# Experts of a mixture layer: 39 tiles of 128 rows in place of 23 tiles of 256

## The reference

```
logits = xf @ Wr.T                       # 2048 tokens, 8 experts
scores, expert = top_k(logits, 2)
weights = softmax(scores)
for e in range(8):
    h = silu(xf @ Win[e].T)              # 256 -> 512
    y += gate[:, e:e+1] * (h @ Wout[e].T)  # 512 -> 256
```

## Time and profile before

| | |
|---|---|
| median of the runs | 1393.06 us |
| span of the profiled execution | 1390.6 us |
| experts: first transpose to last matmul | 1229.8 to 1365.1 us |
| matmuls recorded in all | 8885 |
| granted TensorE clock, mean | 0.969 |

### The profile page before, as it was taken

How to read it: one execution, slowest core, us unless ns; L and a number is a source line. 1 busy time by engine, 2 the same in 40 slices (tenths; PEclk the granted TensorE clock), 3 DMA queues, 4 the chain that set the end, 5 groups by cost and what they waited for, 6 DMA issues and landing times. The chain is left out here.

```text
span 1390.6 us, 30539 instructions
## 1 busy us (share of the span) xinstructions
PE 1286.4 (93%) x8885; PEld 938.2 (67%) x8885; DVE 1054.3 (76%) x2477; ACT 925.3 (67%) x3621; POOL 743.8 (53%) x1099
## 2 busy tenths in 40 slices
PE   3899999999996999999999999999899999669992
PEld 2234444544345888888888888888787878559992
DVE  6456666666676888888888889888788888746664
ACT  1245555454567899899988998899788878323331
POOL 2354646464646556655665566556455788313331
PEclk9799999999998999999999999999999999879996
DMA  5442323233212202202220122112221101522325
GB/s 136 114 76 56 72 55 68 60 59 70 47 51 65 80 2 81 81 13 67 80 80 23 57 80 80 31 48 80 81 81 54 40 32 36 232 88 78 93 82 184
DMA packets 145819, 100.49 MB, mean 72 GB/s; under 512 B 68541, under 2 KB 139198, under 8 KB 145728
## 3 DMA queue, kind: packets, MB, share of 16 engines
q1 hardware_dynamic: 134592, 87.28, 23.5%
q0 software_dynamic: 3744, 8.45, 1.7%
q10 hardware_dynamic: 7392, 3.64, 0.9%
HBM read 58.42 MB, written 42.48 MB: 73 GB/s over the span
## 5 line engine op out<-in xcount | busy, mean ns | idle before, releaser
L1430 POOL TENSOR_TENSOR head_rstd<-head_rstd,minus_half 128x4 f32<-128x4 f32 x192 | 224.8, 1171 | 15.1
L1418 ACT ACTIVATE squares<-ps 128x128 bf16<-128x128 f32 x768 | 201.8, 284 | 46.3 <-PE ps L1381 36.5
L1381 PE MATMUL ps<-w_proj_in,xq 128*128 128x512 f16 (+1 forms) x1024 | 210.1, 328 | 7.0 <-ACT headsT L1454 6.4
L1510 POOL TENSOR_TENSOR prob<-prob,rinv 128x512 f32<-128x512 f32 x128 | 138.4, 1081 | 107.7 <-DVE rinv L1505 107.4
L1497 ACT ACTIVATE prob<-ps,nmax 128x128 f32<-128x128 f32 x512 | 182.2, 390 | 10.3 <-DVE nmax L1488 9.0
L1454 ACT ACTIVATE headsT<-ps,l_hln 128x256 f32<-128x256 f32 (+1 forms) x256 | 167.8, 688 | 31.7 <-PE ps L1445 31.7
L1418 ACT ACTIVATION_READ_ACCUMULATOR squares<-ps 128x1 f32 x768 | 165.2, 216 | 0.0
L1438 DVE TENSOR_TENSOR heads_n<-ps,head_rstd 128x512 f32<-128x512 f32 x192 | 131.3, 684 | 25.0 <-POOL head_rstd L1430 24.8
L728 DVE TENSOR_REDUCE nmax<-ps 128x4 f32<-128x512 f32 x128 | 85.1, 683 | 73.2 <-PE ps L721 73.0
L1481 PE MATMUL ps<-headsT 128*128 128x128 f32 x1024 | 136.5, 276 | 1.0 <-DVE probT L1526 0.4
L1381 PEld LDWEIGHTS ps<-w_proj_in,xq 128*128 (+1 forms) x1024 | 100.5, 98 | 53.9 <-issue 8.2
(11 more groups left out here) (304 smaller groups left out, 2797.3 us busy)
## 6 DMA issues: line engine op xcount, KB each, us to landing
slots<-blank_slot SPq DMA_DIRECT2D x12, 1554.0 KB, 8.8
halves<-half_made SPq DMA_DIRECT2D x32, 256.0 KB, 2.6
w_proj_in<-halves SPq DMA_DIRECT2D x16, 512.0 KB
taken<-slots SPq DMA_DIRECT2D x23, 259.0 KB, 2.8
w_out_raw<-in_wprojT SPq DMA_DIRECT2D x8, 512.0 KB, 3.8
half_raw<-in_winT SPq DMA_DIRECT2D x16, 256.0 KB, 3.0
half_raw<-in_woutT SPq DMA_DIRECT2D x16, 256.0 KB, 3.1
q_stack<-q_parts SPq DMA_DIRECT2D x48, 64.0 KB
```

The source lines that it names most:

```text
L1381: last = e.matmul(out, xq[:, k, which, slot_at], weights(k, hl, c0, n), start=(k == 0 and hl == 0), stop=(k == KD - 1 and hl == 1))
L1418: last = e.activation(squares[:, 4 * n + h, :], A[n][:, h * HD1:(h + 1) * HD1], ACT.Square, scale=HD1**-0.5, accum_out=hss[:, 4 * n + h:4 ...
L1430: e.tensor_tensor(hr[:, four], hr[:, four], t["half"][:, four], ALU.pow).then_inc(g_r[n].sem, 1)
L1510: e.tensor_tensor(prob[:, kind, :, :], prob[:, kind, :, :], spread(rinv[:, kind, :], P), ALU.mult).then_inc(g_p[kind].sem, 1)
```

## The change

`TS` becomes 1, so a tile has 128 rows and there are 2 x 16 + 7 = 39 tiles. A tile's inner layer (4 x 128 columns) now fits one PSUM bank, so four tiles have a bank each, with one activation, one cast and one subtraction of 512 columns a tile. `hidden` runs two tiles ahead of `down` in place of one. `xT`, `h32` and `hh` have four places, the rings of `taken`, `y` and the notes six. The tables of tiles grow from 24 to 40 entries (three words of experts to five), by `TILES`.

```
-TS = 2
+TS = 1
-    RING = 3
+    RING, DEEP = 6, 4
-    xT = sb("slotsT", [P, 2, 2 * KD, TR], F16)
-    h32, hh = sb("h32", [P, 2, KF, TR]), sb("hidden", [P, 2, 2, KF, TR], F16)
+    xT = sb("slotsT", [P, DEEP, 2 * KD, TR], F16)
+    h32, hh = sb("h32", [P, DEEP, KF, TR]), sb("hidden", [P, DEEP, 2, KF, TR], F16)
...
         def hidden(n):
             e.wait_ge(s_xT, n + 1)
+            if n >= len(Hb):
+                e.wait_ge(s_h, n - len(Hb) + 1)
             mine = expert(n)
             for m in range(KF):
-                if n >= 2 and m % 2 == 0:
-                    e.wait_ge(s_h, 2 * (n - 2) + m // 2 + 1)
...
-                        last = e.matmul(Hb[2 * (n % 2) + m // 2][:, m % 2 * TR:(m % 2 + 1) * TR], w,
-                                        xT[:, n % 2, part * KD + k, :],
+                        last = e.matmul(Hb[n % len(Hb)][:, m * TR:(m + 1) * TR], w, xT[:, n % DEEP, part * KD + k, :],
...
-                if m % 2:
-                    last.then_inc(s_H, 1)
+            last.then_inc(s_H, 1)

         def down(n):
             mine = expert(n)
             if n >= 2:
                 e.wait_ge(s_y, n - 1)
-            for h in range(TS):
-                for m in range(KF):
-                    if h == 0 and m % 2 == 0:
-                        e.wait_ge(s_hh, 4 * n + 2 * (m // 2) + 2)
+            e.wait_ge(s_hh, 2 * n + 2)
+            for m in range(KF):
...
-        turn(0)
-        turn(1)
+        for n in range(3):
+            turn(n)
         e.wait_ge(t["weights_in"], 16 * 2 * LOADS)
         hidden(0)
+        hidden(1)
         for n in range(TILES):
-            if n + 1 < TILES:
-                hidden(n + 1)
             if n + 2 < TILES:
-                turn(n + 2)
+                hidden(n + 2)
+            if n + 3 < TILES:
+                turn(n + 3)
             down(n)
...
-        lift(0)
-        lift(1)
+        for n in range(3):
+            lift(n)
         for n in range(TILES):
             parts(n)
             aim(n)
+            if n + 3 < TILES:
+                lift(n + 3)
...
+        silu(0)
+        silu(1)
+        for n in range(TILES):
             if n + 2 < TILES:
+                silu(n + 2)
```

More of the change, by code:

```diff
@@ L2181, in down @@
                 e.wait_ge(s_y, n - 1)
-            for h in range(TS):
-                for m in range(KF):
-                    if h == 0 and m % 2 == 0:
-                        e.wait_ge(s_hh, 4 * n + 2 * (m // 2) + 2)
[L2186 to L2189, removed]
+            e.wait_ge(s_hh, 2 * n + 2)
+            for m in range(KF):
+                for part, hl in ((0, 0), (0, 1), (1, 0)):
+                    w = wout[:, hl, bass.ds(mine, 1), m, :].rearrange("p e n -> p (e n)")
+                    last = e.matmul(Yb[n % 2][:, 0:D], hh[:, n % DEEP, part, m, :], w,
+                                    start=(m == 0 and part == hl == 0), stop=(m == KF - 1 and part == 1))
             last.then_inc(s_Y, 1)
-        turn(0)
-        turn(1)
+        for n in range(3):
+            turn(n)
         e.wait_ge(t["weights_in"], 16 * 2 * LOADS)
         hidden(0)
+        hidden(1)
         for n in range(TILES):
-            if n + 1 < TILES:
-                hidden(n + 1)
             if n + 2 < TILES:
-                turn(n + 2)
+                hidden(n + 2)
+            if n + 3 < TILES:
+                turn(n + 3)
             down(n)
@@ L2206, in lift @@
             e.wait_ge(s_turn, n + 1)
-            if n >= 2:
-                e.wait_ge(s_H, 2 * (n - 1))
-            e.tensor_copy(xT[:, n % 2, :, :].rearrange("p c t -> p (c t)"), turned[n % 2][:, :]).then_inc(s_xT, 1)
+            if n >= DEEP:
+                e.wait_ge(s_H, n - DEEP + 1)
+            e.tensor_copy(xT[:, n % DEEP, :, :].rearrange("p c t -> p (c t)"),
+                          turned[n % 2][:, 0:2 * KD * TR]).then_inc(s_xT, 1)
         def aim(n):
@@ L2235, in parts @@
         def parts(n):
[L2236 to L2244, removed]
+            if n >= DEEP:
+                e.wait_ge(s_Y, n - DEEP + 1)
+            e.wait_ge(s_h, n + 1)
+            e.tensor_copy(hh[:, n % DEEP, 0, :, :], h32[:, n % DEEP, :, :]).then_inc(s_hh, 1)
+            e.wait_ge(s_hh, 2 * n + 1)
+            e.tensor_tensor(hh[:, n % DEEP, 1, :, :], h32[:, n % DEEP, :, :], hh[:, n % DEEP, 0, :, :],
+                            ALU.subtract).then_inc(s_hh, 1)
         e.tensor_scalar(gate[:, :], gates[:, 3:4], 1.0 / W_UP, None, ALU.mult).then_inc(s_gate, 1)
-        lift(0)
-        lift(1)
+        for n in range(3):
+            lift(n)
         for n in range(TILES):
@@ L2251, in _ @@
             aim(n)
-            if n + 2 < TILES:
-                lift(n + 2)
+            if n + 3 < TILES:
+                lift(n + 3)
     @block.scalar
@@ L2257, in silu @@
         def silu(n):
[L2258 to L2263, removed]
+            e.wait_ge(s_H, n + 1)
+            if n >= DEEP:
+                e.wait_ge(s_hh, 2 * (n - DEEP) + 2)
+            e.activation(h32[:, n % DEEP, :, :].rearrange("p k t -> p (k t)"), Hb[n % len(Hb)][:, :],
+                         ACT.Silu, scale=1.0 / W_UP).then_inc(s_h, 1)
         silu(0)
+        silu(1)
         for n in range(TILES):
-            if n + 1 < TILES:
-                silu(n + 1)
+            if n + 2 < TILES:
+                silu(n + 2)
             e.wait_ge(s_Y, n + 1)
```

## The result

The changed kernel takes 1398.73 us (median of 7 runs, 1397.95 to 1400.43), beside 1393.68 for the kernel before (7 runs, 1390.16 to 1395.96). The recorded ratio is 1.0044, interval [1.003, 1.0058] (the two medians alone give 1.0036). The interval leaves 1 out, but the difference is under the 0.5% that the prediction took as the least that can be told from no change. The forecast was 1395.1, with 1387 to 1408 as its range. The profiled execution took 1396.1 us against 1390.6.

What follows compares the result with a forecast made beforehand. The array bounds the kernel before; with small tiles TensorE's sequencer would, at 3.49 us a tile. End +3.7 and tail -1.65 give +2.1 on the profiled 1390.6, 1392.7; with 2.5 for median over span, 1395.1 us, range 1387 to 1408.

Steps and rivals of the forecast that it cites:

- The sequencer becomes the bound: Experts stage: with small tiles TensorE's sequencer, still issuing 16 + 8 register instructions, needs 3.49 us against the array's 2.88.
- Array work 2.88 us a tile: TensorE, experts: 28 x 0.056 + 12 x 0.109 us; 39 tiles make 112.3 us against 130.9, 18.6 less.
- Rival 1: Experts stage: the array stays the bound, the sequencer costing less or overlapping; tile 2.88 us, 1373.7 us in all; 12%.
- The sequencer's tile of 3.49 us: TensorE's sequencer: 2.14 for `hidden`, 1.02 for `down`, 0.33 for waits; lower end 3.27, upper end 3.87.
- Start: Stage start: `hidden(0)` stands behind three transposed tiles and is issued at 1232.75 against 1232.0, 0.75 us later.
- End: Stage end: the last two `down` run at the array's slower pace; PE ends at 1368.8 against 1365.08, +3.7 us.
- Tail: Behind PE's end: one scaling on ACT and one indirect DMA of POOL, in place of two each; -1.65 us.
- The lift: VectorE's lift, one tile ahead: a 1.17 us chain beside 1.35 us of sequencer work, slack 0.18, so no wait.
- Rival 2: Sequencer's wait for `s_xT` in `hidden(n+3)`: the lift becomes late; 1402 to 1410 us, likeliest 1403; 25%.
- Depth worth nothing: Forecast for the follow-up runs: `hidden` one tile ahead instead of two makes no difference, within 0.3%, at either bound.
- The rule on weight loads at 128 columns: TensorE: load and matmul pairs sustain about 81 ns, giving 3.58 us a tile, 1398.6; 6% together with a 1417 us case.
- The clock: TensorE: a rival had the clock fall because of small array gaps; 5.4 us a tile, over 1460 us; 2%.

Runs made afterwards that it cites:

- paired: Changed kernel with the addresses of two weight blocks (high and low part) worked out together ahead of their three matmuls, in `hidden` and `down`: 1374.67 us, ratio 0.988.

## Why the prediction held, point by point

- *The sequencer becomes the bound*: right. The register instructions are 16 and 8, 0.124 us apart in the plain case. With 9 and 4 in their place the kernel gains some 23 us, with 16 more it loses some 55.
- *Array work 2.88 us a tile*: right; 2.87 where it is the bound (paired, and with fixed addresses). Rival 1's time of 1373.7 is what these gave (1374.67 and 1373.78): of the 18.6 us of array work that the smaller tiles save, 17 show once the sequencer is out of the way. In the changed kernel it takes them back.
- *The sequencer's tile of 3.49 us*: the term that was mis-sized. It is 3.58. By the trace's starts, means over 35 tiles: `hidden` 15 x 0.138 + 0.13 = 2.20 us (2.14 forecast), `down` 7 x 0.131 + 0.13 = 1.05 (1.02), waits 0.106 + 0.106 + 0.131 = 0.34 (0.33). The greater part of the 0.09 is in `hidden` (0.06). On 39 tiles 0.09 us is 3.5 us. Two errors partly cancelled. The 0.127 came from two stretches of 16 that already held the long first interval (0.205 and 0.188 us by the trace's starts, the plain ones 0.124), and the sum then added 0.11 for the first once more. Left out were the late starts: behind the first, one interval in nine in `hidden` (60 of 548) and one in twelve in `down` (23 of 273) is longer than 0.145, up to 0.28. The range had room for it (3.27 to 3.87).
- *Start*: forecast 0.75 later; the first `hidden` is issued at 1232.24, 0.5 earlier than forecast. 0.3 of that is chance of the execution, whose first transposes start at 1229.50 in place of 1229.80. *End*: PE ends at 1372.22 in place of 1368.8, 3.4 later: the 3.5 less those 0.5, and some 0.4 that isn't accounted for. *Tail*: -1.65 forecast, -1.6 measured. Net +2.1 forecast, +5.5 measured; what is missing is, nearly all of it, the sequencer's 0.09 us a tile.
- *The lift*: it takes 0.42 us as forecast and starts 0.04 behind the transposes' end. POOL misses it as worked out: counted from `hidden`'s wait (1293.67 by the trace's starts) POOL starts at 1.88 us (1295.55; forecast 1.95) and the lift at 2.93 (1296.60; forecast 2.95). The slack of 0.18 was wrong, and on the side of the lift's chain: the sequencer has 1.37 us of work beside it (1.35 forecast), but from the transposes' wait (1292.41) to the lift's end (1293.35) it is 0.94 and with 0.05 back 0.99, not 1.17, since the transposes start 0.10 behind the wait's start where I had 0.27. That leaves 0.38, and the extra copy of 0.34 fitted in. Rival 2 had its 25% for a slack half as large as it is, and no run came near its case until two copies were added (0.27 us a tile, where 0.68 less 0.38 is 0.30).
- *Depth worth nothing*: right, at both bounds.
- *The rule on weight loads at 128 columns*: the Trainium skill (TensorE: Matmul & The Clock Gate, Back-to-back issue gap) has about 81 ns each for a stream of such pairs. `hidden` in the changed kernel runs at a mean of 85 ns, so by the mean the rule seems to be met. It isn't what happens: two of three starts there are 0.06 us apart and the third 0.124, where the prediction named even spacing as the sign of this rival, and without register instructions 24 such pairs run at 56 ns. The measurement decides. Two explanations gave 1395.1 and 1398.6, and the time measured (1398.73) lay on the wrong one by chance; the single starts and the experiments tell them apart, the time doesn't.
- *The clock*: 1.00 between 1244 and 1358, as before. The array idles for a fifth of the time, in gaps of 0.03 us between matmuls in the mean, and this did not lower it.

## What to carry to other kernels

When tiles get smaller, what is paid per weight block stays: count the sequencer's register instructions for each matmul, and compare their spacing with the array's. Busy time of PE hides it, and so does a mean: read the single starts. Compare part by part (`hidden` by itself), and not only over the tile. Where an address is known only at run time, work out several in one instruction ahead of the matmuls that use them; here this turned a change worth nothing into 17 us (1.2%).

## What was not expected of the hardware

- A register instruction with three address operations in it holds TensorE's sequencer for 0.124 us, whether one or two pairs of weight load and matmul follow. With six it is 0.152. Moving one of the three into an instruction of its own costs 0.088 more. A wait that is already met: 0.106 us to the register instruction behind it.
- Starts of register instructions are sometimes 0.02 to 0.16 us late, which adds up, with the long first one, to some 0.27 us a tile over the plain spacing (3.58 against 15 x 0.124 + 0.124 + 0.126 + 0.106 + 8 x 0.124 + 0.106 = 3.31). 0.1 of it is the first one in each `hidden`, which is recorded as 0.162 us long and also works out the expert. The rest has a pattern: where two starts in one `hidden` are late, they lie 32 instructions of TensorE's program apart (register instructions, weight loads and matmuls counted), in 22 of 22 cases in the changed kernel and 23 of 23 with `down` paired. So the lateness seems to come with every 32nd instruction, and smaller tiles, which have more instructions for each row, would meet it more often. What it is stays open; no run varied it.
- In the paired kernel POOL's indirect DMA runs beside VectorE's cast, and most casts there (33 of 38) take some 0.57 us in place of 0.42:

```profile
1292.33 0.97 POOL L2287 DMA_INDIRECT picked<-slots_y,to_row  x1 [1.90 <-DVE to_row L2225]
...
1292.99 0.57 DVE L2244 CAST hidden<-h 128x512 f16<-128x512 f32 x1
```

  There the cast starts 0.66 us behind the start of the DMA. In the paired kernel that works one tile ahead it starts 0.79 behind and takes 0.43, and where only `down` is paired 0.84 or more behind, and takes 0.42. So running side by side isn't enough: in these runs it goes by where in the DMA the cast begins.

  The tile stays at 2.87 us in the paired kernel, but VectorE is busy for 85.88 of 96 us in its stretch from 1244 to 1340 us, so it stands nearest behind the array:

```profile
1244.00:1340.00 96.00, 96.00 (x1335) 91.42 (x1334) 85.88 (x300) 35.62 (x68) 32.53 (x34) 1.00 0.29 86
```
